# Scale of the normalisations in three parts; mixtures' weights loaded by SyncE and prepared in the last patch unit

## What is computed

```python
h = gelu(patches(x) @ weight + bias)
h = h + relu_attention(norm(h))          # scores masked, relu, divided by row
h = h + mixture0(norm(h))                # 6 experts of 3 layers, the best 2
h = h + rope_attention(norm(h))          # causal softmax
h = h + mixture1(norm(h))                # 8 experts of 2 layers, the best 2
# norm(h) = (h - mean) / sqrt(var + 1e-5), over the 64 of each vector
```

## Time and profile before

| | |
|---|---|
| median of 3 runs | 668.27 us (664.47 to 670.48) |
| the profiled execution | 667.97 us, its span 666.2 us |
| TensorE matmuls, busy | 591.1 us, 89% of the span |
| VectorE, busy | 505.0 us, 76% |
| ScalarE, busy | 297.6 us, 45% |
| GpSimd, busy | 148.0 us, 22% |
| mean granted clock of TensorE | 0.959 of full speed |

### The profile page before, as it was taken

One profiled execution on the slowest core, in us unless ns is written; L12 is line 12 of the kernel. 1 busy time (PEld: TensorE's weight loads), 2 busy tenths in 40 slices (PEclk: granted clock), 3 DMA queues, 4 the chain that ended last, 5 costly groups with the idle time before them and its releaser, 6 DMA issues.

```text
span 666.2 us, 17580 instructions
## 1 busy us (share of the span) xinstructions
PE 591.1 (89%) x6943; PEld 369.3 (55%) x6943; DVE 505.0 (76%) x1493; ACT 297.6 (45%) x716; POOL 148.0 (22%) x151
## 2 busy tenths in 40 slices
PE   1899999899998799999988889999967879999883
PEld 1885655468887344445443358777764444444441
DVE  3657779848785769888787548878887888988863
ACT  0010010023334466776775648887852434545441
POOL 1000000853655103221011041531421122121000
PEclk9999999999989799999998999999975899999997
DMA  9999883000000000000000000000000000000001
GB/s 296 411 384 331 292 292 132 2 1 1 2 1 2 1 1 1 3 1 1 2 1 1 1 2 1 1 2 2 1 1 1 7 16 22 22 22 21 20 22 25
DMA packets 28898, 39.19 MB, mean 59 GB/s; under 512 B 19985, under 2 KB 20369, under 8 KB 28817
## 3 DMA queue, kind: packets, MB, share of 16 engines
q1 hardware_dynamic: 19232, 35.46, 15.0%
q10 hardware_dynamic: 9584, 2.61, 2.0%
HBM read 35.37 MB, written 2.69 MB: 57 GB/s over the span
## 4 chain that ended last, share of the span: by engine, by line
PE 55%; DVE 24%; issue 7%; ACTq 6%; ACT 5%; DMA 2%; SPq 0%; DVEq 0%
PE bank L1522 8%; PE bank L403 7%; ACTq L1192 6%; DVE m_hm L1783 4%; PE bank L1560 4%; PE bank L1042 2%; PE bank L1558 2%; PE bank L1583 2%; PE bank L992 2%; PE bank L1006 2%; PE bank L1543 2%; PE bank L785 2%; PE bank L771 2%; DVE cols L446 2%; PE bank L1532 2%
## 5 line engine op out<-in xcount | busy, mean ns | idle before, releaser
L558 POOL TENSOR_TENSOR centred<-h,mean 82x512 f32<-82x512 f32 x64 | 72.8, 1137 | 447.3 <-DVE rstd L541 236.9
L1403 ACT ACTIVATE m_h<-bank,m_b 128x656 f32<-128x656 f32 x112 | 90.5, 808 | 115.6 <-PE bank L1522 115.4
L403 PE MATMUL bank<-cols,tok_weight 64*64 64x328 f32 (+1 forms) x1800 | 114.8, 410 | 20.2 <-DVE cols L447 18.3
L1783 DVE TENSOR_TENSOR m_hm<-bank,m_h 128x656 f32<-128x656 f32 x112 | 93.7, 836 | 34.3 <-PE bank L1532 33.0
L403 PEld LDWEIGHTS bank<-cols,tok_weight 64*64 64x64 f32 x1800 | 75.4, 135 | 55.1 <-issue 17.5
L1522 PE MATMUL bank<-m_xt,m_w 64*64 64x328 f32 x896 | 92.5, 485 | 5.9 <-ACT m_h L1403 5.0
L446 DVE COPY cols<-image 128x1992 f32<-128x1992 f32 x32 | 62.0, 1945 | 16.9 <-DMA image<-in_x_dram 14.8
L1558 PE MATMUL bank<-m_hm,m_wo 64*64 64x328 f32 x512 | 49.3, 455 | 2.7 <-DVE m_osb L1790 2.3
L1522 PEld LDWEIGHTS bank<-m_xt,m_w 64*64 64x64 f32 x896 | 24.8, 137 | 45.8 <-issue 23.2
L952 ACT ACTIVATE sa_prob<-sa_masked,sa_low 82x82 f32<-82x82 f32 x128 | 44.6, 350 | 11.3 <-DVE sa_low L1094 11.2
L381 ACT ACTIVATE tok_fm<-bank,tok_bias 128x328 f32<-128x328 f32 x16 | 7.6, 532 | 88.9 <-PE bank L403 63.1
(11 more groups left out here) (170 smaller groups left out, 1026.0 us busy)
## 6 DMA issues: line engine op xcount, KB each, us to landing
image<-in_x_dram SPq DMA_DIRECT2D x32, 1000.0 KB, 11.1
out_dram<-m_fin SPq DMA_DIRECT2D x16, 164.0 KB
tok_weight<-in_L_tok_weight_dram ACTq DMA_DIRECT2D x2, 400.0 KB, 8.1
m_w<-in_L_ffn_w_dram ACTq DMA_DIRECT2D x2, 128.0 KB
m_sel_raw<-c_sel_dram ACTq DMA_DIRECT2D x1, 256.0 KB
m_w<-in_L_ffn_expert_w_dram ACTq DMA_DIRECT2D x2, 96.0 KB
m_wo<-in_L_ffn_expert_w_dram ACTq DMA_DIRECT2D x4, 48.0 KB
m_sel_raw<-c_sel_dram ACTq DMA_DIRECT2D x1, 192.0 KB
```

The lines of the kernel that those rows point to most:

```text
L403: return pe.matmul(sum_bank[u % 2][s][t * D:(t + 1) * D, L * j0:L * j1], weight[s * R:(s + 1) * R, c, :], cols[u % 2][s * R:(s + 1) * R, c ...
L558: pool.tensor_tensor(self.centred[:], slots(self.h, g), mean.broadcast_to([L, G, D]), ALU.subtract).then_inc(self.shifted, 1)
L1403: act.activation(h1[n % RING][:], h1_bank, ACT.Gelu if last else ACT.Relu, bias=W.b1[:, k:k + 1]).then_inc(h1_ready, 1)
L1783: dve.tensor_tensor(hm[k][:], cb_bank, src[n % RING][:], ALU.mult).then_inc(hm_ready, 1)
```

## The change

- `scale` takes a part: groups 0 to 7, 8 to 11 or 12 to 15 (`ends`). Every group's statistics raise `counted`, and `normalise` waits for the part that its group needs.
- A part has 14 instructions in place of 17. One polynomial step takes the place of the first two Newton steps, with a factor that the last step takes up; three instructions no longer wait for the one before (`mark`). It still yields in 6 pieces.
- Placing: part 0 of the first normalisation in units 5 and 6, part 1 at the end of unit 7, whole. In the first attention part 2 in groups 2 to 7, a piece each, in the second in groups 1 to 6; the next one's part 0 in groups 9 to 11, two pieces each. First mixture: parts 1 and 2 in groups 1, 2 and 4, 5, a piece before each `weigh`, the next one's part 0 in groups 10 to 12 and its part 1 in groups 14 and 15. Last mixture: part 1 in group 0 in two lots of three pieces, part 2 in groups 2 to 4 in three lots of two; `count_last` in group 1.
- The loads of both mixtures are issued by SyncE behind the last image, and both are prepared in unit 7, in front of `store(6)`.

```diff
@@ stage_patches
         in_groups(step)
+        for W in moe:
+            W.load(sp)
...
-            for W in LOAD_IN.get(u, ()):
-                (*attn, *moe)[W].load(act)
+            if u == 0:
+                for W in attn:
+                    W.load(act)
...
+            if u == NU - 1:
+                for W in moe:
+                    W.prepare(dve)
             if u >= 1:
                 store(u - 1)
                 statistics(2 * u - 2)
...
-            if u in PREPARE_IN:
-                moe[PREPARE_IN.index(u)].prepare(dve)
-            if u in (4, 5):
+            if u in SCALE_IN:                 # (5, 6)
                 go(scale, 3)
+        go(following.scale(dve, 1))
         yield
         store(NU - 1)
@@ LayerNorm
+    def scale(self, dve, part):
+        first, end = ((0,) + self.ends)[part:part + 2]
+        cols = slice(G * first, G * end)
...
+        dve.wait_ge(self.counted, end)
         if self.previous is not None:
+            dve.wait_ge(self.previous.normed, end)
+        self.mark(dve.scalar_tensor_tensor(q, self.stats[:, cols, 2], EPS * D, self.stats[:, cols, 5], ALU.add, ALU.add))
         self.link(dve, dve.tensor_tensor(d, even, odd, ALU.subtract))
+        yield
+        self.mark(dve.scalar_tensor_tensor(self.mean[:, cols], d, -0.5, even, ALU.mult, ALU.add))
         self.link(dve, dve.scalar_tensor_tensor(var, d, float(n * n) / D / D, d, ALU.mult, ALU.mult))
...
+        self.link(dve, dve.tensor_tensor(q, d, d, ALU.mult))
+        self.link(dve, dve.tensor_tensor(q, q, var, ALU.mult))
+        yield
+        self.link(dve, dve.scalar_tensor_tensor(q, q, -10.0 / 3, q, ALU.add, ALU.mult))
+        self.link(dve, dve.scalar_tensor_tensor(d, q, 5.0, d, ALU.add, ALU.mult))
+        yield
+        self.link(dve, dve.tensor_tensor(q, d, d, ALU.mult))
+        self.link(dve, dve.scalar_tensor_tensor(q, q, -0.5 * 0.375 ** 3, var, ALU.mult, ALU.mult))
+        dve.scalar_tensor_tensor(self.rstd[:, cols], q, 1.5 * 0.375, d, ALU.add, ALU.mult).then_inc(self.scaled, 1)
...
-        pool.wait_ge(self.scaled, 2 if g >= NG // 2 else 1)
+        pool.wait_ge(self.scaled, 1 + sum(end <= g for end in self.ends))
@@ first attention (the second: 1 <= g <= 6)
-            if 1 <= g <= 3:
-                go(scale_mine, 2)
-            if 9 <= g <= 10:
-                go(scale_next, 3)
+            if 2 <= g <= 7:
+                go(scale_mine, 1)
+            if 9 <= g <= 11:
+                go(scale_next, 2)
@@ mixtures, last and first
+        SCALE_MINE, SCALE_NEXT, COUNT_LAST = ({(0, 2): 3, (0, 3): 3}, {(2, 3): 2, (3, 2): 2, (4, 3): 2}), (), (1, 2)
...
+        SCALE_MINE = {(g, k): 1 for g in (1, 2) for k in range(NP)}, {(g, k): 1 for g in (4, 5) for k in range(NP)}
+        SCALE_NEXT = {(g, k): 1 for g in (10, 11, 12) for k in (0, 1)}, {(g, k): 1 for g in (NG - 2, NG - 1) for k in range(NP)}
+        COUNT_LAST = (0, LAST)
```

More of the change, by code:

```diff
@@ L43 @@
 NBLOCK = L + (PW - 1) // SW
-LOAD_IN, MULTIPLY_IN, PREPARE_IN = {0: (0, 1), 1: (2,), 2: (3,)}, (2, 3), (4, 5)
+MULTIPLY_IN, SCALE_IN = (2, 3), (5, 6)
 RING = 3
@@ L176, in build @@
         for i in range(4):
-            norm.append(LayerNorm(sem, f"ln{i}", shared, xn[i % 2], i % 2 == 0, norm[-1] if i else None))
+            norm.append(LayerNorm(sem, f"ln{i}", shared, xn[i % 2], i % 2 == 0, norm[-1] if i else None, (NG // 2, 3 * NG // 4, NG)))
         with ExitStack() as inner:
@@ L494, with __init__ @@
 class LayerNorm:
-    def __init__(self, sem, name, shared, xn, halves, previous):
+    def __init__(self, sem, name, shared, xn, halves, previous, ends):
         self.h, self.stats, self.mean, self.rstd, self.tmp, self.centred = shared
@@ L501, in __init__ @@
         self.previous = previous
+        self.ends = ends
         self.counted = sem(name + "_counted")
@@ L546, in count_last @@
             ins = dve.bn_stats(slot(self.stats, NG - 1, b), slot(self.h, NG - 1, b))
-        self.link(dve, ins)
+        ins.then_inc(self.counted, 1)
     def rows(self, g):
@@ L820, in vector @@
     def vector(dve):
-        scale_mine, scale_next = mine.scale(dve, 1), following.scale(dve, 0)
+        scale_mine, scale_next = mine.scale(dve, 2), following.scale(dve, 0)
         for i, t in enumerate(pt):
@@ L834, in statistics @@
                 ins = dve.bn_stats(slot(stats, g, b), slot(h, g, b))
-            if g == NG // 2 - 1:
-                ins.then_inc(following.counted, 1)
+            ins.then_inc(following.counted, 1)
         def weigh(g):
@@ L1139, in vector @@
                 mine.count_last(dve)
[L1140 to L1143, removed]
+            if 1 <= g <= 6:
+                go(scale_mine, 1)
+            if 9 <= g <= 11:
+                go(scale_next, 2)
             yield
@@ L1802, in statistics @@
                 ins = dve.bn_stats(slot(stats, g, b), slot(h, g, b))
-            if g == NG // 2 - 1:
-                ins.then_inc(following.counted, 1)
-        scale_mine, scale_next = mine.scale(dve, 1), None if last else following.scale(dve, 0)
+            ins.then_inc(following.counted, 1)
+        scale_mine = [mine.scale(dve, part) for part in (1, 2)]
+        scale_next = [] if last else [following.scale(dve, part) for part in (0, 1)]
         take_logits(0)
@@ L1843, in step @@
                     residual(g - 1)
[L1844 to L1847, removed]
+                for part, pieces in enumerate(SCALE_MINE):
+                    go(scale_mine[part], pieces.get((g, k), 0))
+                for part, pieces in enumerate(SCALE_NEXT):
+                    go(scale_next[part], pieces.get((g, k), 0))
                 weigh(g, k)
-            if g == 0:
-                mine.count_last(dve)
+                if (g, k) == COUNT_LAST:
+                    mine.count_last(dve)
         in_groups(step)
```

18 lines of the change are left out of this document (5 added, 13 removed).

## The result

The changed kernel takes 676.24 us (median of 4 runs, 675.40 to 677.66) where the kernel before takes 669.38 beside it: a ratio of **1.0168**, 95% interval 1.0118 to 1.0217. The forecast of 660 and its range, 653 to 671, were both wrong. The profiled span is 674.3 for 666.2, 8.1 more. (676 is also the figure of rival A, loads that land late. That is a coincidence: no load is waited for, as the rows show.)

The account below looks back on a forecast made before the run. The prediction took TensorE as the bound (55% of the chain of waits; VectorE 24%). Terms 1.2 - 1 + 2.4 + 0.8 + 1.0 + 3.5 = 7.9 us, off 667.97, gave 660, range 653 to 671.

Parts of the forecast that it names:

- rival A: Patch stage's end: weight loads on SyncE land late, at 150, delaying the second prepare; 676 us, chance 0.12.
- The patch stage: Units 4 to 6: all three TensorE waits go, so unit 7 ends at 139.5, 5.3 us earlier.
- The 2 to land: Weight loads on SyncE: estimated 2 us from the last issue at 131.5 to landing, giving 134.
- The last unit on VectorE: Unit 7: prepares, store, scale and memset put the first pt at 147.4; only 1.2 of the 5.3 us is left.
- The rule quoted from the Trainium skill: Unit 7: GpSimd contends with VectorE for SBUF interfaces; by it part 1 of scale would take 7.8 us.
- B: Rival: gains given back through half clock around the first attention and a last mixture gaining only 1; 665.5 us, chance 0.19.
- Clock: TensorE's clock after its wait of 4 us before the first attention: a loss of 1 us, bounds 0 and 2.
- First attention, 2.4: First attention: both waits for pt go and the mixture's first transposition starts earlier; 1.07 + 1.3 = 2.4 us gained.
- First mixture, 0.8 gained: First mixture: shorter scale pieces over more groups leave about half of the 2.0 us waits for m_hm; 0.8 gained.
- The part at groups 14 and 15 fits into idle VectorE: First mixture's end: the next scale's part 1 fits in VectorE's idle time there; no separate cost in the sum.
- Second attention, 1.0: Second attention: the wait of 0.99 us behind scale bursts at groups 9 and 10 goes; 1.0 gained.
- Last mixture, 3.5: Last mixture: scale and statistics moved into VectorE's idle pieces bring outputs closer; 3.5 us gained, bounds 0 and 5.

Follow-up runs that it names:

- kernel 6: The changed kernel with GpSimd's first normalisation waiting until both layers are prepared in unit 7: 672.28 us, ratio 1.0087.
- kernel 1: The changed kernel with the mixtures' loads back on ScalarE and their prepare back in units 4 and 5, new scale kept: 663.31 us, ratio 0.9955.
- kernel 5: The changed kernel with loads on ScalarE, prepare in units 4 and 5, and the next scale's early part in group 14 alone: 657.31 us, ratio 0.9868.
- Kernel 9: kernel 5 with the mixture's first part of scale in the first attention's groups 9 and 10, three pieces each: 657.67 us, ratio 0.9882.
- Kernel 8: kernel 5 with the last mixture's own scale parts and last count back at their old places: 665.55 us, ratio 0.9993.
- kernel 7: kernel 5 with the first mixture's own scale parts spread thinner, two pieces per group in groups 0 to 5: 658.03 us, ratio 0.9886.
- kernel 4: The changed kernel with the first mixture's part 1 of the next scale in group 14 alone, none in group 15: 669.85 us, ratio 1.0082.

## Why the prediction was wrong

**The patch stage was right.** Unit 7 ends at 139.75 (forecast 139.5), `scaled` comes at 128.6 (128.3), and the last load is issued at 131.1 (131.5). The 2 to land stood in no row of before, whose image loads take 4.7 at least; kernel 6 shows 2.0 after the last issue. Of the 5.3 gained, 1.45 is the wait for ScalarE that kernels 1 and 5 do not have either.

**The step that failed is "The last unit on VectorE"**, in two sentences of it. "With one such hold for each of GpSimd's 6 instructions" the first `prepare` was to end at 134. The six holds were there and brought it to 135.7. At the text's own price, 0.73 each, they make 4.4 and an end at 135.5, so 1.5 of the error is in that sum (and part 1 with every second step held would be 8.4, not 7.8). What was left out is the memsets directly behind them, which the text did count as GpSimd's work, further on, but as harmless ("GpSimd clears tiles for half of that time"). They held one cast for 4.4 more. "Then come the second `prepare` 2.8" took it for quiet, while the delay had put it beside GpSimd's next two groups: 6.1. Together 6.3 + 3.3 = 9.6 too little. The steps behind it were right, 10.35 from 146.37 to the first `pt` against 10.6. The first `pt` was forecast at 147.4 and came at 156.72.

The rows had the price, 0.95 for 0.22; it was applied to 6 of GpSimd's instructions when 19 stood beside the two `prepare` (three groups, nine memsets, two more groups). The rule quoted from the Trainium skill (GPSIMD Engine Reference, 1. Specifications) was used on `scale` alone. There its warning did not come true: part 1 took 4.4, not 7.8, since GpSimd stood waiting for TensorE until 151.83. It came true on `prepare`, 18 of whose 20 steps are small casts and sums in the SBUF. None of the rivals had this mechanism; B came nearest (a wait that brings the lower clock), with a price of 1.

**Clock.** Forecast 1 lost. The two waits were 6.37 and 4.03, not 4 in one piece, and the clock was at 0.67 and 0.59 over the 19 behind and between them. It is part of the 9.1.

**First attention, 2.4.** Gained in full (2.5) up to the last transposition, then 2.0 given back in front of the mixture: GpSimd's group comes late behind the third group of pieces, the wait of 1.85. The text had put the late `scaled` at 1.3 gained. Of the wait of 1.51 for `pt`, which was to go, 0.73 is left, at 198.90. Kernel 9 removes the wait and gains nothing that can be measured: the wait stood in front of others, of 1.08 and more.

**First mixture, 0.8 gained.** It lost 1.9. "Shorter pieces over more groups leave about half" did not come true: waits for `m_hm` 2.5, before 2.0. Groups 3 to 5 take 2.1 more than before and groups 1 and 2 take 0.6 less. Another 0.6 lies in front of the first output, where the lower clock plays in and where kernels 5 and 8, alike up to there, differ by 2.6 (46.2 and 43.6 from the first transposition), so it proves nothing. There were 17 steps of the mixture's own `scale` and there are now 28; at 32 columns one takes 0.19 where it takes 0.22 at 64, so to split a part in two makes it 1.7 times as long. That the number of steps is the cause is argued, no kernel had them in one part; the rows of kernel 7 speak for a second cause, GpSimd's groups, which each `scaled` releases beside the routing.

**"The part at groups 14 and 15 fits into idle VectorE".** It nearly does in 14, where the first three pieces cost 0.4 (8.83 between outputs for 8.43) and all six 0.6 (9.02 in kernel 4), and not in 15: 4.4, shown by kernels 4 and 5. This idle time was not looked up in a row.

**Second attention, 1.0:** 1.1. **Last mixture, 3.5:** 5.8, over its bound of 5. Right mechanism, size too small: behind the first output 3.3 is gained, near the forecast, and 2.4 in front of it, where TensorE's waits for `pt` and `m_hm` fell from 3.24 and 1.32 to 2.12 and none. The clock has a part in this: before, TensorE fell to the lower one once more at 526.10 (1.08 for four matmuls, 0.64 after), which the text had not priced. Kernel 8 loses 6.0 behind the first output against kernel 5, but 3.1 of that is what kernel 5 gains over the kernel before.

In sum: -7.9 forecast and +8.1 measured differ by 16.0; 9.3 lies in the last unit with its clock, 2.0 in the first attention, 2.7 in the first mixture, 4.4 at its end, and the second attention and the last mixture take 2.4 off.

Left open: why the memset run held one cast for 4.60 in the changed kernel, and in kernel 4, at the same place, for 2.38, with the rest falling on the two steps behind. And how much of the 9.1 is the clock's: no kernel had these waits at full clock.

## What to carry to other kernels

Before small SBUF-to-SBUF steps are moved on VectorE, write down, instruction by instruction, what GpSimd does at the new place, memsets included; a `prepare` of 2.8 became 11.8. If the delay itself pushes the next steps beside GpSimd's next work, count that too. And "idle" needs a row for the very group in which a step is put: all six pieces cost 0.6 in group 14, three of them cost 4.4 in group 15, and the last mixture gained 5.8 where an idle stretch had been looked up. An earlier `scaled` is not free either: it starts GpSimd's next groups, and they may meet other small steps (kernel 7).

## What the runs showed of the hardware

- A run of memsets on GpSimd, with no gap between them, can hold one VectorE cast or `tensor_scalar` over several of them: 4.60, 3.56, 3.36 and 2.40 for steps of 0.18 or 0.19 (3.56 and 3.36 began beside the normalising instruction just ahead). Steps with two SBUF inputs were not held beside memsets (0.19 and 0.22).
- The hold goes both ways. In the kernel before, GpSimd's first three instructions took 2.62, 2.71 and 4.59 beside VectorE's copies of the images (1.04 in quiet), and two of VectorE's copies of two columns took 1.02 and 1.01 for 0.15.
- Issues of the same 54 loads took 29.3 on SyncE's queue with nothing else to do, 46.5 on ScalarE's with images streaming (41.8 in kernel 1); the two loads of `m_b` in pieces of four bytes took 0.64 each, where they took 0.75 and 4.79.
- Each kernel has a stretch at the lower clock near the entrance to the first mixture, behind short waits of TensorE, and its place and length vary: 0.60 over 12.9 from 225.5 in the kernel before, 0.85 and 0.83 over 21.3 from 222.7 in kernel 4. The runs of one kernel spread with the mean clock: kernel 5 took 654.4 at 0.969 and 659.2 at 0.962.
